# A two-layer attention network on one core: the order of work in the first layer's two attentions

## What is computed

```python
# block 0 (block 1 has a feed-forward after each of its attentions, and head size 16)
x = attn(ln(x, g1, b1), ln(x, g1, b1), Wq1, Wk1, Wv1, Wo1, bo1) + x     # self: 512 keys
x = attn(ln(x, g2, b2), context, Wq2, Wk2, Wv2, Wo2, bo2) + x           # cross: 1601 keys
x = geglu(ln(x, g3, b3), Wp, bp, Wf, bf) + x

def attn(xq, xc, Wq, Wk, Wv, Wo, bo):
    q, k, v = (xq @ Wq, xc @ Wk, xc @ Wv)           # each split into 16 heads
    scores = einsum('bnhd,bshd->bhns', q, k) * scale
    out = einsum('bhns,bshd->bnhd', softmax(scores), v)
    return out @ Wo + bo
```

## Time and profile before

| | |
|---|---|
| median of 3 runs | 3445.59 us (3444.46 to 3449.68) |
| span of the profiled execution | 3432.5 us |
| the profiled execution's own time | not given beside its span |
| TensorE busy | 3202.0 us, 93% of the span, 17084 matmul records |
| VectorE busy | 2266.1 us, 66% |
| ScalarE busy | 1823.8 us, 53% |
| GpSimd busy | 1087.6 us, 32% |
| mean granted TensorE clock | 0.957 of full speed |

### The profile page before, as it was taken

One profiled execution on the slowest core, in us unless ns is written; L12 is line 12 of the kernel. 1 busy time (PEld: TensorE's weight loads), 2 busy tenths in 40 slices (PEclk: granted clock), 3 DMA queues, 4 the chain that ended last, 5 costly groups with the idle time before them and its releaser, 6 DMA issues. The chain is left out here.

```text
span 3432.5 us, 48146 instructions
## 1 busy us (share of the span) xinstructions
PE 3202.0 (93%) x17084; PEld 1837.0 (54%) x17084; DVE 2266.1 (66%) x4098; ACT 1823.8 (53%) x3369; POOL 1087.6 (32%) x537
## 2 busy tenths in 40 slices
PE   7969996999979999999999989979999699999989
PEld 5834443888834444444444457733468444444347
DVE  5447774444357666666666555569766599999844
ACT  4424444444424444444444434447766268888864
POOL 1036663000037777777777720002200000000000
PEclk9979998999979999999999999979999789999999
DMA  6888884999785766676667442154544723323140
GB/s 233 306 201 222 227 216 176 362 346 352 281 206 132 160 152 141 140 162 150 142 141 162 117 162 105 71 171 132 193 172 167 251 71 107 104 90 113 59 142 28
DMA packets 367126, 588.79 MB, mean 172 GB/s; under 512 B 47152, under 2 KB 197216, under 8 KB 365736
## 3 DMA queue, kind: packets, MB, share of 16 engines
q1 hardware_dynamic: 361710, 582.41, 57.4%
q10 hardware_dynamic: 5178, 3.31, 0.4%
HBM read 344.19 MB, written 241.29 MB: 171 GB/s over the span
## 5 line engine op out<-in xcount | busy, mean ns | idle before, releaser
L2253 ACT ACTIVATE a_prob<-a_ring 128x512 f32<-128x512 f32 (+1 forms) x1088 | 575.4, 601 | 656.8 <-PE a_ring L2161 587.4
L2279 DVE TENSOR_REDUCE a_blk_max<-a_ring 128x1 f32<-128x402 f32 x1024 | 519.4, 567 | 321.2 <-PE a_ring L2145 321.1
L1790 ACT ACTIVATE a_prob<-a_ring 128x512 f32<-128x512 f32 (+1 forms) x1088 | 582.1, 605 | 136.3 <-PE a_ring L1712 131.1
L2102 POOL TENSOR_TENSOR a_prob_sum<-a_prob,a_prob_sum 128x1024 f32<-128x1024 f32 x256 | 600.6, 2385 | 3.1 <-ACT a_prob L2253 3.1
L2174 PE MATMUL a_pv<-a_prob,a_v 128*64 128x512 f32 (+1 forms) x2176 | 534.5, 610 | 0.0
L1835 DVE TENSOR_REDUCE a_blk_max<-a_ring 128x1 f32<-128x402 f32 x1024 | 506.7, 567 | 33.4 <-PE a_ring L1699 27.0
L2160 PE MATMUL a_ring<-a_q_stack,a_k_stack 128*128 128x512 f32 (+1 forms) x1088 | 463.4, 426 | 13.5 <-DMA a_q_second<-maxima 13.4
L2161 PE MATMUL a_ring<-a_q_second,a_k_second 65*128 65x512 f32 (+1 forms) x1088 | 435.2, 400 | 0.0
L2102 POOL TENSOR_TENSOR a_prob_sum<-a_prob 128x1024 f32<-128x1024 f32 x128 | 302.7, 2375 | 416.7 <-DVE a_chunk_sum L2310 242.7
L1730 PE MATMUL a_pv<-a_prob,a_v 128*32 128x256 f32 (+2 forms) x4096 | 340.7, 406 | 13.6 <-ACT a_prob L1790 7.8
L1699 PE MATMUL a_ring<-a_k_stack,a_q_stack 63*128 63x402 f32 (+1 forms) x1280 | 281.9, 423 | 39.2 <-DMA a_q_stack<-q_lo_self 18.7
(11 more groups left out here) (268 smaller groups left out, 4676.3 us busy)
## 6 DMA issues: line engine op xcount, KB each, us to landing
a_k_stack<-k_hi_cross SPq DMA_DIRECT2D x96, 400.5 KB, 4.6
a_v<-v_cross SPq DMA_DIRECT2D x48, 768.0 KB
a_k_stack<-k_lo_cross SPq DMA_DIRECT2D x80, 400.5 KB, 6.0
a_k_second<-k_hi_cross SPq DMA_DIRECT2D x32, 801.0 KB, 12.5
v_cross<-p_v_sb SPq DMA_DIRECT2D x48, 512.0 KB
k_hi_cross<-p_split_hi SPq DMA_DIRECT2D x120, 200.0 KB, 3.4
k_lo_cross<-p_split_lo SPq DMA_DIRECT2D x120, 200.0 KB, 4.3
a_q_stack<-q_hi_self SPq DMA_DIRECT2D x64, 256.0 KB, 4.2
```

The lines of the kernel that those rows point to most:

```text
L1790: nc.scalar.activation(prob[0:keys, tau % RC, m, :], ring[0:keys, score_place(e) % BANKS, :], ACT.Exp, scale=a.scale).then_inc(exp_done, 1)
L2102: nc.gpsimd.tensor_tensor(prob_sum[:, h], prob_of(i * NCP + cp, h), other, ALU.add)\
L2253: nc.scalar.activation(prob_of(w, h)[0:keys, ch % 2, :], ring[0:keys, score_bank(e), :], ACT.Exp, scale=a.scale).then_inc(exp_done, 1)
L2279: nc.vector.reduce_max(dst, ring[:, max_bank(g), 0:a.blk], AX.X).then_inc(item_read, 1)
```

## The change

The order of both attentions is made of stretches (`stints`): in a0 a stretch is a whole group (4 chunks), in a1 four stretches make a group, with 2, 4, 4 and 3 chunks. TensorE's order in a stretch is all its scores, two pairs of maxima, the values of the stretch before, in some stretches the sums, and then the rest of the maxima. In a0 the row of maxima of group i + 2 is stored in group i and loaded in group i + 1; row 1 is now handled by SP. The late steps of VectorE and ScalarE are placed by stretch. RC becomes 4 in both; in a1 OS becomes 2, `o_raw` has one buffer, and `den` lies in `chunk_sum`. SP's stores of results in a1 come one group later. NM is the number of stretches of a group, NS of the stage.

```diff
-    RC = 3 if a.cross else 4
-    OS = 3 if a.cross else 4
+    RC = 4
+    OS = 2 if a.cross else 4
+    RB = 1 if a.cross else 2
...
+    stints = [[0], [1, 2], [3, 4], [5, 6]] if a.cross else [[0, 1]]
+    NM = len(stints)
+    NS = NG * NM
+    def units(k):
+        return [k // NM * NCP + cp for cp in stints[k % NM]]
+    def pairs_by(k):
+        ahead_by, ramp = ((10, 14, 18, 22), 6) if a.cross else ((10,), 10)
+        steady = PAIRS * (k // NM + 1) + ahead_by[k % NM]
+        return min(NG * PAIRS, steady, PAIRS + ramp * (k + 1))
+    def cut(k):
+        return min(pairs_by(k), pairs_by(k - 1) + 2)
...
         # SP
+            if not a.cross:
+                store_maxima(1)
+                load_maxima(1)
...
-                    at(store, i - 1)
+                    at(store, i - 2)
...
         # TensorE
-            def sums_at(w):
-                if w >= DEN_AT and (w - DEN_AT) % NCP == 0 and (w - DEN_AT) // NCP < NG:
-                    denominators(pe, (w - DEN_AT) // NCP)
+            def sums_at(k):
+                if a.cross and k >= 5 and k % NM == 1:
+                    denominators(pe, (k - 5) // NM)
+                elif not a.cross and k:
+                    denominators(pe, k - 1)
...
-            for w in range(T):
-                for ch in a.pair(w % NCP):
-                    for h in range(2):
-                        scores(w, ch % 2, h)
-                maxima(pairs_by(w - 1), cut(w))
-                if w:
-                    values(w - 1)
-                sums_at(w)
-                maxima(cut(w), pairs_by(w))
+            for k in range(NS):
+                for w in units(k):
+                    for ch in a.pair(w % NCP):
+                        for h in range(2):
+                            scores(w, ch % 2, h)
+                maxima(pairs_by(k - 1), cut(k))
+                if k:
+                    for w in units(k - 1):
+                        values(w)
+                sums_at(k)
+                maxima(cut(k), pairs_by(k))
...
         # ScalarE, for w in range(T)
-                if cp == 1 and i:
+                if a.cross and cp == 1 and i:
                     raw_copy(i - 1)
+                elif not a.cross and cp == 0 and i >= 2:
+                    raw_copy(i - 2)
...
-                if not a.cross and cp == NCP - 1 and i + 1 < NG:
-                    load_maxima(i + 1)
                 for ch in a.pair(cp):
-                    if ch == a.pair(cp)[-1] and w >= HIGH_AT and (w - HIGH_AT) % NCP == 0:
-                        high_part((w - HIGH_AT) // NCP)
...
-                if not a.cross and cp == NCP - 2 and i + 1 < NG:
-                    store_maxima(i + 1)
+                if not a.cross and cp == 0 and 1 <= i < NG - 1:
+                    load_maxima(i + 1)
+                elif not a.cross and cp == 1 and i < NG - 2:
+                    store_maxima(i + 2)
+                if cp == 4 and i:
+                    high_part(i - 1)
+                elif cp == NCP - 1 and not a.cross and i >= 2:
+                    high_part(i - 2)
...
         # VectorE
+            def behind_scores(k):
+                if not a.cross:
+                    at(low_part, k - 2)
+                elif k % NM == 2:
+                    at(invert, k // NM - 1)
+                    at(divide, k // NM - 1)
+            def behind_values(k):
+                if not a.cross:
+                    at(turn_sums, k - 1)
+                    at(invert, k - 1)
+                    at(divide, k - 1)
+                elif k % NM == 0:
+                    at(last_sum, k // NM - 1)
+                    at(last_merge, k // NM - 1)
+                elif k % NM == 1:
+                    at(turn_sums, k // NM - 1)
+                elif k % NM == 2:
+                    at(low_part, k // NM - 1)
+                if ahead and k < NS:
+                    for m in ahead.early:
+                        if m + NCP in units(k):
+                            ahead.rest_of_piece(dve, m)
...
+            for k in range(NS + NM + (0 if a.cross else 1)):
+                if k < NS:
+                    blocks(pairs_by(k - 1), cut(k))
+                behind_scores(k)
+                if k < NS:
+                    blocks(cut(k), pairs_by(k))
+                behind_values(k)
```

More of the change, by code:

```diff
@@ L2176, in values @@
                     last.then_inc(pv_done, 1)
-            def sums_at(w):
-                if w >= DEN_AT and (w - DEN_AT) % NCP == 0 and (w - DEN_AT) // NCP < NG:
-                    denominators(pe, (w - DEN_AT) // NCP)
-            maxima(0, pairs_by(-1))
-            for w in range(T):
-                for ch in a.pair(w % NCP):
-                    for h in range(2):
-                        scores(w, ch % 2, h)
-                maxima(pairs_by(w - 1), cut(w))
-                if w:
-                    values(w - 1)
-                sums_at(w)
-                maxima(cut(w), pairs_by(w))
-            values(T - 1)
-            if not ahead:
-                for w in range(T, T + DEN_AT):
-                    sums_at(w)
+            def sums_at(k):
[3 more added lines that the diff above has]
+                    denominators(pe, k - 1)
+            maxima(0, pairs_by(-1))
+            for k in range(NS):
+                for w in units(k):
+                    for ch in a.pair(w % NCP):
[7 more added lines that the diff above has]
+                maxima(cut(k), pairs_by(k))
+            for w in units(NS - 1):
+                values(w)
+            if not a.cross:
+                sums_at(NS)
         @block.scalar
@@ L2254, in _ @@
                                              ACT.Exp, scale=a.scale).then_inc(exp_done, 1)
[L2255 to L2256 removed]
+                if not a.cross and cp == 0 and 1 <= i < NG - 1:
[7 more added lines that the diff above has]
+            if not a.cross:
+                raw_copy(NG - 2)
+                high_part(NG - 2)
             raw_copy(NG - 1)
[L2258 to L2259 removed]
+            high_part(NG - 1)
         @block.vector
@@ L2323, in low_part, with at @@
                     .then_inc(o_lo_done, 1)
-            def late(step, half, at):
-                if half >= at and (half - at) % (2 * NCP) == 0 and (half - at) // (2 * NCP) < NG:
-                    step((half - at) // (2 * NCP))
+            def at(step, i):
+                if 0 <= i < NG:
+                    step(i)
+            def behind_scores(k):
+                if not a.cross:
+                    at(low_part, k - 2)
+                elif k % NM == 2:
+                    at(invert, k // NM - 1)
+                    at(divide, k // NM - 1)
@@ new lines, in behind_values @@
+            def behind_values(k):
+                if not a.cross:
+                    at(turn_sums, k - 1)
[12 more added lines that the diff above has]
+                            ahead.rest_of_piece(dve, m)
+                if ahead and k == NS - 1:
+                    for m in ahead.late:
+                        ahead.rest_of_piece(dve, m)
@@ L2330, in _ @@
             dve.wait_ge(pad_set, 1)
             blocks(0, pairs_by(-1))
-            for half in range(2 * (T + HIGH_AT + 1)):
-                w = half // 2
-                if ahead and half % 2 and w - NCP in ahead.early:
-                    ahead.rest_of_piece(dve, w - NCP)
-                elif ahead and half == 2 * T - 1:
-                    for m in ahead.late:
-                        ahead.rest_of_piece(dve, m)
-                if half % 2 == 0:
-                    blocks(pairs_by(w - 1), cut(w))
-                else:
-                    blocks(cut(w), pairs_by(w))
-                late(turn_sums, half, TURN_AT)
-                if dve_sums:
-                    late(last_sum, half, SUM_AT)
-                    late(last_merge, half, MERGE_AT)
-                late(invert, half, INVERT_AT)
-                late(divide, half, DIVIDE_AT)
-                late(low_part, half, LOW_AT)
+            for k in range(NS + NM + (0 if a.cross else 1)):
[5 more added lines that the diff above has]
+                behind_values(k)
```

35 lines of the change are left out of this document (13 added, 22 removed).

## The result

Before and after were run five times each on one chip. Before: 3430.59 to 3449.68 us, median 3445.59. After: 3408.78 to 3418.57 us, median 3414.96. The ratio is 0.9925 with a 95% interval of 0.9905 to 0.9946, so the change makes the kernel faster, by 19 to 33 us. The forecast was 3426 with 3398 to 3442.

A forecast was written before the change was run, and what follows sets the result against it. It took TensorE's order of work to bound the cross attention and a chain of waits the self attention. -35 + 11 + 5 = -19 us against the 3432.5 span gives 3413.5, plus 13.1 beside the span: 3426, range 3398 to 3442.

The forecast's parts named there:

- The forecast case: Whole kernel: 3426 us, with a range of its own of 3411 to 3438, chance 0.72.
- the term for the time beside the span: Whole kernel: the median before, 3445.6, is 13.1 us above the span of 3432.5; carried onto the predicted span.
- The cross attention, by the sum of its blocks: Cross attention: fewer changes of matmul kind, 31.29 to 30.18 us a group; 35 us saved, bounds 31 to 37.
- The collision in the second group: Second cross attention group: VectorE's weight pieces wait for GpSimd's additions; 11 us lost, between 4 and 16.
- the 10.389 us row: Late weight piece in the profile before, held over several GpSimd additions; taken as reason to expect more than 4 us.
- The 10 us hole in TensorE: Sign of being right: one such hole in the second cross group, beside a VectorE piece lasting many us.
- The self attention: A chain of waits through VectorE, ScalarE and TensorE sets the period: 11.15 against 10.6, 15.5 us lost; net +5.
- the 4.6 gained at the end: End of the self attention: last values fill TensorE's 4.68 us wait for GpSimd's last merge; 4.6 us gained.
- The start: Start of the self attention: rows of groups 1 and 2 have a stretch more; 6 us gained, bounds 0 and 10.
- the first rival: Self attention's chain doesn't bind: period 9.75 instead of 11.15, 39 us less, 3387; half of that, 3407; chance 0.15.
- The store's landing: Rival, self attention: the landing of the maxima store holds ScalarE; 3468 at 8 us, 3445 at 7.2; chance 0.08.
- The fixed parts: Rival, cross attention: fixed parts of blocks are not saved but moved into longer blocks; -35 becomes 0, 3461; chance 0.05.

The follow-up runs named there:

- Experiment 4: Changed kernel with stretches of one chunk pair in the cross attention, seven in a group, so the old block counts return; one run, 3438.37 us.
- experiment 2: Changed kernel with VectorE splitting the four early weight pieces one per group, just ahead of the last sum, when GpSimd's additions have ended; one run, 3400.09 us.
- experiment 6: Edits 1 and 2 together, plus GpSimd waiting before its fifth addition in a1's last group until all six pieces are divided; median 3366.92 us, ratio 0.9792 to before.
- experiment 1: Changed kernel with ScalarE's high half ahead of the store and load of maxima in the self attention; median 3377.74 us, ratio 0.982 to before.
- edits 1 and 2 together: Changed kernel with the edits of experiment 1 and experiment 2 both made; median 3371.71 us, ratio 0.9803 to before.
- experiment 3: Changed kernel with the self attention back in the order of before, so the change stands in the cross attention alone; one run, 3410.59 us.
- experiment 5: Changed kernel with all four pairs of maxima of a cross attention stretch in one block between scores and values; one run, 3517.08 us.
- experiment 7: Changed kernel plus probes: VectorE adds a 128 x 16 tile to itself after the second, third and fourth stretch of a1's groups; one run, 3662.44 us.
- experiment 8: Experiment 7's probe after the second and third stretch alone, behind 0 to 8 short one-input VectorE instructions to vary its moment; one run, 3645.72 us.

## Why the prediction was right

The forecast case came in, at a median 11 us below its number. The 11 us are the term for the time beside the span. The sum of the stages came out within 4 us, by two mechanisms that were right and, in the cross attention, by two misses that cancel.

**The cross attention, by the sum of its blocks: right.** Predicted 30.18 a group, measured 30.15; predicted 31.29 for before, measured 31.28. Experiment 4 takes the blocks back and the gain goes. From the first maxima of a1 to the feed stage the prediction had -35 + 11 = -24; the traces show -24.7. From first to last call of the sums a1 took 27.5 us less with the collision in it, so the blocks gave about -34. The agreement in the total is luck: the collision below cost 6.3 and not 11, and from the first maxima to the first sums a1 took 75.0 us where it had taken 71.9 (966.03 to 1041.04, and 961.55 to 1033.46), for which the sum has no term. In experiment 2 that same part took 70.7. TensorE was idle in it for 7.8 and 7.5 us, and lost 21.1 and 16.4 us to a lower granted clock, so it is the clock that differs; no run says why.

**The collision in the second group: there, but of the shorter kind, and the term mis-sized.** I took 11 us between bounds of 4 and 16; it was 6.3 (experiment 2). The step that failed is the choice by the 10.389 us row: here VectorE got in at the next boundary both times. The 10 us hole in TensorE that was to show it right did not come either; its longest gap there is 1.91. And the sum priced waiting alone: it has no term for TensorE's clock, which fell to half behind that gap and cost 3.4 of the 6.3 us. The Trainium skill (SBUF — State Buffer, Who interferes with whom) has the later instruction wait until the first finishes; by that alone it was 4 us, and for the wait at this place (the 2.9 us that the clock leaves of the 6.3) it was the better guide. For the late pieces it was not: in five of the ten profiled executions without experiment 6's wait (before, after, experiments 1 and 4, edits 1 and 2 together) the first late piece took 9.9 to 14.9 us across several additions, in the other five (experiments 2, 3, 5, 7 and 8) 2.3 to 3.4. The prediction used the late row for the early pieces and gave the late pieces themselves no term. In the changed kernel's profile they cost 8 us against experiments 2 and 3 (last two calls of the sums 34.5 apart against 26.1). They had cost about as much before, where the last two calls of the sums are 34.25 apart (34.5 after), so the difference of the two profiles doesn't show it.

**The self attention: right, in its chain and nearly so in its ends.** Predicted period 11.15 with 1.4 us of waiting, released by the low half; measured 11.24 with 1.24, released by it. Experiment 1 removes the link named and only that. Over 27 periods the calls of the sums take 303.2 us where they took 287.9, 15.3 more; the term says 15.5 for 28. Before the last sums TensorE waits 0.58 us where it waited 4.68, so 4.1 of the 4.6 gained at the end are there. The start is harder to read. The first sums come 12.6 us sooner (227.96 against 240.52), where I took 6, but they also stand behind less work: 64 matmuls of maxima and scores and 16 of values, where the old order had done 80 and 32. Counted at equal work (each matmul at its distance in its block), the new order is about 4 us ahead there, an estimate. Net +6.3 at the last sums and +4.5 at the first maxima of a1, against a predicted +5. The prediction also put the period without the store's hold at 10.6 "nothing lost", and the first rival at 9.75; experiment 1 gives 9.85, since the high half, once in front, waits for no row at all.

**The 13.1 us around the span: wrong.** I carried the distance of the median (3445.6) from the span (3432.5) as time beside the span. Every execution listed since took 1.8 more than its span. The execution profiled before was one of the quick ones, about 3434.3 by that, in a kernel whose runs scatter from 3430 to 3450. Without this term the sum is 3413.5 + 1.8 = 3415.3, against a median of 3415.0 and a profiled execution of 3418.6. This agreement is partly luck: the untouched rest took 4.5 us more in this profile, and between 1436 and 1447 us in the others.

**The rivals.** The self attention's chain does bind (11.24, not 9.8). The store's landing did not hold ScalarE: the load was issued at 332.71, 5.9 us behind its store, between the third exponential and the fourth, which follow each other without a stop (three from 331.38 for 1.58, five from 332.82). The fixed parts were saved. The slower side didn't come.

## What to carry to other kernels

Where TensorE is busy without a gap, count its changes from one kind of matmul to another and price them from its own timeline; this sum was right to 0.1%. Where it isn't, follow the closed chain of waits through all engines, and look in it for an instruction that is merely queued behind somebody else's wait: here the high half behind the issue of a store, worth 37 us for a few lines that change places. Don't place a VectorE instruction with two SBUF inputs where GpSimd has several ready additions in a row, or let GpSimd wait for it. Price a stall of a dense TensorE stream by more than its length: here gaps of 1.9 and 4.4 us each brought about as much again, or more, in a halved clock behind them. And compare a profile's span with the span of another execution, not with a median.

## What the runs showed of the hardware that I had not expected

- A VectorE instruction with two inputs in SBUF can be passed over by GpSimd at each boundary between two additions, up to the end of its run: 8.9 us for an instruction of 0.16. Of the 116 probes asked for inside a run, 57 were held to its end (5.2 to 10.3). The others waited at most 2.12, to the next boundary. GpSimd lost nothing to the probes (eight additions in 18.67 us, 18.65 before) and about 1 us to each whole piece that got in; VectorE's reads of maxima out of PSUM ran beside its additions in their usual 2.03 for four.
- Which of the two happens went with the place in the run and not with the moment within an addition in 115 of the 116 probes (experiments 7 and 8: third or fourth addition let in, sixth to eighth held). The weight pieces don't follow it: one asked for in the seventh addition got in, and the first late piece, asked for 0.1 to 0.2 us into the fifth addition of ten in seven of the kernels, was held in three of them (the changed one, experiment 1, edits 1 and 2 together) and let in at the next boundary in four (experiments 2, 3, 7 and 8). This stays open, and with it how much of the scatter of 10 us between runs of one kernel is these 8 us.
- TensorE's granted clock fell to half behind stalls of a few us in a stream that was busy without a gap before: for 6.8 us behind the gap of 1.91 in the second group, for 10.24 us behind nearly all of the 28 gaps of 4.33 to 4.44 in experiment 7. Without a stall it stayed at 1.00 through the regular groups.
- The untouched stages behind a1 differed by up to 10 us between kernels (1436.4 to 1447.0), with the same 9016 matmuls before as after. TensorE is idle there for 98 to 100 us in all eleven profiles. What differs is the time lost to a lower granted clock (the length times one minus the mean granted share): 61.4 us in the shortest, 71.7 and 75.5 us in the two longest, with a correlation of 0.92 over all eleven. Why the clock differs, no run here says.
